# Row maxima of the global scores carried as eight more contraction rows, with local and global units taken in turn

## What is computed

```python
x = x + pos_emb[:S]                          # of the layer norm of x
w = x.reshape(B, nW, WIN, H, hd)             # WIN = 128, so 2 windows; 16 heads of 16
local = softmax(einsum('bnqhd,bnkhd->bnhqk', w, w) * scale) @ w
comp = conv1d(x, conv_w, stride=4) + conv_b  # 64 compressed positions
gt = concat([comp, global_memory])           # 64 + 64 global positions
glob = softmax(einsum('bshd,bghd->bhsg', x, gt) * scale) @ gt
mix = sigmoid(concat([local, glob]) @ gate_w + gate_b)
out = (mix * local + (1 - mix) * glob) @ out_w + out_b
```

## Time and profile before

| | us |
|---|---|
| median of 3 runs | 1249.25 |
| lowest and highest of them | 1235.91, 1250.31 |
| profiled execution, its own time | 1245.38 |
| its span, first to last instruction | 1243.6 |
| self-attention, first scores to last projection | about 31.7 to 509 |
| cross-attention | about 510 to 804 |
| experts | about 804 to the end |

### The profile page before, as it was taken

How to read it: one execution, slowest core, us unless ns; L and a number is a source line. 1 busy time by engine, 2 the same in 40 slices (tenths; PEclk the granted TensorE clock), 3 DMA queues, 4 the chain that set the end, 5 groups by cost and what they waited for, 6 DMA issues and landing times.

```text
span 1243.6 us, 29954 instructions
## 1 busy us (share of the span) xinstructions
PE 1134.6 (91%) x11749; PEld 981.6 (79%) x11749; DVE 593.2 (48%) x1187; ACT 518.3 (42%) x833; POOL 542.7 (44%) x651
## 2 busy tenths in 40 slices
PE   3699999999999998799998988999979989999995
PEld 2578787878788787577776776799978889999995
DVE  1355556555556654578886868632313212122221
ACT  1355555554545554377775766621112111111110
POOL 6434343444344222244455555446553444444442
PEclk9699999999999999799999988999989999999998
DMA  6472634435261612266555664479885768888882
GB/s 206 133 183 68 162 93 118 128 83 156 56 168 52 172 54 79 77 166 179 150 128 129 156 155 124 154 212 224 215 201 177 217 207 222 248 235 237 247 231 47
DMA packets 207737, 194.29 MB, mean 156 GB/s; under 512 B 62746, under 2 KB 164863, under 8 KB 207600
## 3 DMA queue, kind: packets, MB, share of 16 engines
q1 hardware_dynamic: 189408, 170.86, 48.3%
q0 software_dynamic: 15840, 18.77, 8.5%
q10 hardware_dynamic: 2352, 2.75, 0.7%
HBM read 152.25 MB, written 40.08 MB: 155 GB/s over the span
## 4 chain that ended last, share of the span: by engine, by line
PE 31%; DMA 17%; DVE 4%; issue 2%; ACT 1%; SPq 1%; POOL 1%; POOLq 0%; DVEq 0%; ACTq 0%
PE ps_scores L1640 11%; DMA out<-y,slot_row 11%; PE ps_out L1658 6%; PE ps_turn L1509 3%; DMA out<-y,out_row 3%; PE ps_misc L1541 2%; PE ps_scores L1496 2%; PE ps_out L1521 2%; DMA q_stack<-q_scr 2%; DMA q_scr<-qp 1%; PE ps_misc L1462 1%; DVE y L2102 1%; PE ps_scores L1489 1%; PE ps_misc L1529 1%; PE ps_turn L1625 1%
## 5 line engine op out<-in xcount | busy, mean ns | idle before, releaser
L1640 PEld LDWEIGHTS ps_scores<-xgT,w 128*128 128x128 f32 x2272 | 265.8, 193 | 5.0 <-ACT xgT L1855 0.7
L1640 PE MATMUL ps_scores<-xgT,w 128*128 128x128 f32 x2272 | 267.3, 277 | 0.7 <-ACT xgT L1855 0.5
L792 ACT ACTIVATE sa_probs<-ps_scores 128x1024 f32<-128x1024 f32 x128 | 131.0, 1023 | 153.6 <-PE ps_scores L521 153.6
L1861 ACT ACTIVATE silu<-ps_scores 128x512 f32<-128x512 f32 x71 | 42.4, 597 | 354.3 <-PE ps_scores L1640 354.3
L1658 PE MATMUL ps_out<-w2s,gate 128*128 x560 | 137.4, 390 | 15.2 <-DVE y L2102 15.2
L2096 DVE TENSOR_TENSOR gate<-ps_scores,silu 128x512 f32<-128x512 f32 x71 | 49.0, 690 | 180.9 <-ACT silu L1861 180.8
L1391 POOL DMA_INDIRECT out<-y,out_row x46 | 72.9, 1584 | 128.2 <-DMA out<-y,out_row 83.4
L1658 PEld LDWEIGHTS ps_out<-w2s,gate 128*128 128x128 f32 x560 | 103.1, 194 | 30.3 <-issue 18.8
L946 DVE TENSOR_REDUCE sa_rowmax<-ps_scores 128x8 bf16<-128x1024 f32 x64 | 78.4, 1224 | 77.4 <-PE ps_scores L507 77.4
L946 DVE TENSOR_REDUCE sa_rowmax<-ps_turn 128x8 bf16<-128x1024 f32 x64 | 78.4, 1225 | 57.5 <-PE ps_turn L512 56.9
L2102 DVE TENSOR_SCALAR y<-ps_out,slot_share 128x256 f32<-128x256 f32 x70 | 33.8, 483 | 133.4 <-DMA out<-y,slot_row 79.7
(11 more groups left out here) (265 smaller groups left out, 2093.4 us busy)
## 6 DMA issues: line engine op xcount, KB each, us to landing
w<-in_w1T SPq DMA_DIRECT2D x71, 512.0 KB, 3.9
w<-in_w3T SPq DMA_DIRECT2D x71, 512.0 KB, 4.9
q_stack<-q_scr SPq DMA_DIRECT2D x96, 128.0 KB
qs<-w_scr SPq DMA_DIRECT2D x24, 256.0 KB, 4.1
ks<-w_scr SPq DMA_DIRECT2D x24, 256.0 KB, 3.9
k_stack<-k_scr SPq DMA_DIRECT2D x48, 120.0 KB, 3.9
w_scr<-wp SPq DMA_DIRECT2D x7, 768.0 KB, 3.7
q_scr<-qp SPq DMA_DIRECT2D x14, 384.0 KB, 4.6
```

The lines of the kernel that those rows point to most:

```text
L792: act.activation(probs[s % 2][:], m.scores[s % 2][:], ACT.Exp, scale=SCALE).then_inc(exped, 1)
L1640: mm = pe.matmul(h_ps[r % 2][:, j, c, :], w13[r % 3][:, j, k, c * P:(c + 1) * P], xgT[r % 2][:, k, :], start=(k == 0), stop=(k == DT - 1))
```

## The change

For global units the order of the two products is turned round. `queries_scores` makes only the product for the maxima, in `turn`. DVE takes the maxima into `rowmax[1]`, now 32 columns wide of which eight are filled. `turn_max` is one matmul with those 32 columns as weights and minus the identity moving. It leaves minus the maxima, turned, on partitions 96 to 127 of the first 128 columns of `scores[1]`. `copy_max` on ACT writes them as bf16 onto eight more rows (96 to 103) of the stacked queries, the 8 x 128 block repeated for each of the eight heads, which is 8 x 1024 elements. `keys_scores` then makes the transposed scores with 104 rows of contraction. The same eight rows of `gs` hold, once and for all, a pattern that picks the head's own maximum, filled by POOL at the start (two copies of 8 x 3072 elements). `subtract_max` stays for the local units.

Units now alternate: n = s // 4, f = s // 2 % 2, kind = s % 2. So `scores[0]` is for local units only and `scores[1]` for global ones, `out` holds both kinds of one half, `outT` gets four buffers, and `turn_back` gathers from two of them. Because `turn` is now in use every second unit, steps that use its halves move: `turn_back(b-1,1,0)` goes behind `keys_scores(b,1)`, `keys_values` stands directly ahead of `queries_scores(b,5)`, `turn_back(b,0,0)` goes two units later. To make room in memory, `mixT` shares `diffT` and `memory` shares a tile of `att`.

Its core, with "..." where lines are left out:

```diff
+    rowmax = [sb(f"sa_rowmax{i}", [P, n], BF16) for i, n in enumerate((HU, 32))]
+    outT = [sb(f"sa_outT{i}", [P, 4, P]) for i in range(4)]
     wk, wv = (sb(n + "_sb", [P, DT, D]) for n in ("WkT", "WvT"))
...
             if p > 1:
-                sp.wait_ge(scored, R * UPR * (p - 1))
+                sp.wait_ge(shifted, R * UPR * (p - 1))
...
+        for i in range(2):
+            pool.wait_ge(pool_set, 10 + i)
+            pool.tensor_copy(gs[i][KS:, :, :].rearrange("j (f h) g -> j f h g", f=DT),
+                             m.ident[KS:KX_ROWS, KS:KX_ROWS].unsqueeze(1).unsqueeze(3).broadcast_to((HU, DT, HU, GK)))\
+                .then_inc(pool_set, 1)
+        pool.wait_ge(pool_set, 12)
         pool.wait_ge(rest_in, N_REST)
         pool.tensor_scalar(gate_b[:], gate_b[:], 0.5, None, ALU.mult).then_inc(bias_set, 1)
...
             n, kind, f = unit(s)
             p, r, U = b // R, b % R, UPR * b + s
             i = p % 2
-            ps = m.scores[s % 2]
...
             if s == 0 and b == 0:
                 for loaded in row0_stacked:
                     pe.wait_ge(loaded, 64)
             elif s == 0:
                 for loaded in w_stacked:
                     pe.wait_ge(loaded, 64 * p + 64)
-            if s == 2:
+            if U > 1:
+                pe.wait_ge(exped, U - 1)
+            for h in range(HU):
+                mm = pe.matmul(m.scores[0][:, h, :], ks[i][:, f * HU + h, r, n * P:(n + 1) * P],
+                               qs[i][0:KS, f * HU + h, r, n * P:(n + 1) * P], start=(h % 4 == 0), stop=False,
+                               skip_group_check=True)
+            mm.then_inc(scored, 1)
+
+        def queries_scores(b, s):
+            n, kind, f = unit(s)
+            p, r, U = b // R, b % R, UPR * b + s
+            i = p % 2
+            if s == 1:
                 for loaded in g_stacked:
                     pe.wait_ge(loaded, 32 * p + 32)
             if U > 1:
+                pe.wait_ge(maxed, U - 1)
+            for h in range(HU):
+                mm = pe.matmul(m.turn[:, h, :], qs[i][0:KS, f * HU + h, r, n * P:(n + 1) * P],
+                               gs[i][0:KS, f * HU + h, r * G:r * G + P], start=(h % 4 == 0), stop=(h % 4 == 3),
+                               skip_group_check=True)
+            mm.then_inc(scored, 1)
+
+        def turn_max(b, s):
+
+            U = UPR * b + s
+            pe.wait_ge(maxed, U + 1)
+            if U > 1:
                 pe.wait_ge(exped, U - 1)
+            else:
+                pe.wait_ge(pool_set, 12)
+            pe.matmul(m.scores[1][KS:, 0, :], rowmax[1][:], m.neg_ident[:], start=True, stop=True,
+                      tile_position=(0, KS), skip_group_check=True).then_inc(max_turned, 1)
+
+        def keys_scores(b, s):
+            n, kind, f = unit(s)
+            p, r = b // R, b % R
+            i = p % 2
+            pe.wait_ge(max_copied, global_unit(b, s) + 1)
             for h in range(HU):
-                mm = pe.matmul(ps[:, h, :], keys(h), queries(h), start=(h % 4 == 0), stop=False,
+                mm = pe.matmul(m.scores[1][:, h, :], gs[i][:, f * HU + h, r * G:r * G + P],
+                               qs[i][:, f * HU + h, r, n * P:(n + 1) * P], start=(h % 4 == 0), stop=(h % 4 == 3),
                                skip_group_check=True)
-            if kind:
-                pe.wait_ge(maxed, U)
-                for h in range(HU):
-                    mm = pe.matmul(m.turn[:, h, :], queries(h), keys(h), start=(h % 4 == 0), stop=(h % 4 == 3),
-                                   skip_group_check=True)
-            mm.then_inc(scored, 1)
+            mm.then_inc(shifted, 1)
 
         def subtract_max(b, s):
 
 
             pe.wait_ge(maxed, UPR * b + s + 1)
             for h in range(HU):
-                mm = pe.matmul(m.scores[s % 2][:, h, :], rowmax[s % 2][:, h:h + 1].broadcast_to((P, P)),
+                mm = pe.matmul(m.scores[0][:, h, :], rowmax[0][:, h:h + 1].broadcast_to((P, P)),
                                m.neg_ident[:], start=False, stop=(h % 4 == 3), skip_group_check=True)
             mm.then_inc(shifted, 1)
 
...
         def turn_back(b, n, kind, bank):
-            o = OPR * b + 2 * n + kind
-            pe.wait_ge(out_copied, o + 1)
-            for g in range(4):
-                mm = pe.transpose(bank[:, g * P:(g + 1) * P], outT[kind][:, g, :], m.ident[:])
+            pe.wait_ge(out_copied, OPR * b + 2 * n + 2)
+            for f in range(2):
+                for g in range(2):
+                    mm = pe.transpose(bank[:, (2 * f + g) * P:(2 * f + g + 1) * P], outT[2 * n + f][:, 2 * kind + g, :],
+                                      m.ident[:])
             mm.then_inc(back_made, 1)
 
         def turn_att(b, n, bank):
...
             if some:
-                scores(b, 1)
+                if old:
+                    pe.wait_ge(att_read, NT * (b - 1) + 1)
+                else:
+                    pe.wait_ge(mem_read, 1)
+                    pe.wait_ge(wT_read, 2)
+                queries_scores(b, 1)
                 subtract_max(b, 0)
             if more:
                 if old:
@@ -621,18 +669,11 @@
                     pe.wait_ge(gT_read, 1)
                 turn_c(b + 1, m.misc)
             if old:
-                turn_back(b - 1, 1, 0, side[1])
                 values(b - 1, UPR - 1)
 
             if some:
-                if old:
-                    pe.wait_ge(att_read, NT * (b - 1) + 1)
-                    pe.wait_ge(back_read, OPR * (b - 1) + 3)
-                else:
-                    pe.wait_ge(mem_read, 1)
-                    pe.wait_ge(wT_read, 2)
                 scores(b, 2)
-                subtract_max(b, 1)
+                turn_max(b, 1)
             if nxt or last and even:
                 pe.wait_ge(cT_read, b + 2)
                 if even:
@@ -644,9 +685,15 @@
                 cross_queries(1)
             if some:
                 values(b, 0)
-
-            if some:
-                scores(b, 3)
+                keys_scores(b, 1)
+                pe.wait_ge(maxed, UPR * b + 2)
+            if old:
+                turn_back(b - 1, 1, 0, side[1])
+
+            if some:
+                if old:
+                    pe.wait_ge(back_read, OPR * (b - 1) + 3)
+                queries_scores(b, 3)
                 subtract_max(b, 2)
             if old:
                 if (nxt or last) and even:
...
-                subtract_max(b, 3)
+                turn_max(b, 3)
             if old:
                 turn_att(b - 1, 1, m.misc)
+            if some:
+                values(b, 2)
+                keys_scores(b, 3)
             if (nxt or last) and even:
                 turn_w(b + 3, side[1])
             if more:
                 keys_values(b + 1, side[0])
-            if some:
-                values(b, 2)
-
-            if some:
-                scores(b, 5)
-                subtract_max(b, 4)
-            if old:
-                gate(b - 1)
+
             if some:
                 if more:
                     pe.wait_ge(k_read, b + 2)
                     pe.wait_ge(v_read, b + 2)
-                turn_back(b, 0, 0, side[0])
-                values(b, 3)
-
-            if some:
-                pe.wait_ge(back_read, OPR * b + 1)
                 if (nxt or last) and even:
                     pe.wait_ge(wT_read, b + 4)
+                queries_scores(b, 5)
+                subtract_max(b, 4)
+            if old:
+                gate(b - 1)
+            if some:
+                values(b, 3)
+
+            if some:
                 scores(b, 6)
-                subtract_max(b, 5)
+                turn_max(b, 5)
+                turn_back(b, 0, 0, side[0])
+                values(b, 4)
+                keys_scores(b, 5)
             if (nxt or last) and even:
                 if old:
                     pe.wait_ge(tanh_done, DT * b)
...
                 else:
                     cross_queries(0)
-            if some:
-                values(b, 4)
-
-            if some:
-                scores(b, 7)
+
+            if some:
+                pe.wait_ge(back_read, OPR * b + 1)
+                queries_scores(b, 7)
                 subtract_max(b, 6)
                 if nxt and even:
                     pe.wait_ge(conv_read, p + 2)
@@ -716,14 +764,13 @@
             if more:
                 scores(b + 1, 0)
             if some:
-                subtract_max(b, 7)
-            if old:
-                if some:
-                    pe.wait_ge(back_read, OPR * b + 2)
+                turn_max(b, 7)
+                values(b, 6)
+                pe.wait_ge(back_read, OPR * b + 2)
+                turn_att(b, 0, side[0])
+                keys_scores(b, 7)
+            if old:
                 project(b - 1)
-            if some:
-                turn_att(b, 0, side[0])
-                values(b, 6)
 
     def scalar_program(act):
...
             act.activation(probs[s % 2][:], m.scores[s % 2][:], ACT.Exp, scale=SCALE).then_inc(exped, 1)
 
```

(95 more changed lines are left out.)

22 lines of the change are left out of this document (11 added, 11 removed).

## The result

Over 20 runs each, the changed kernel took 1254.6 us (1246.2 to 1294.4) and the kernel before 1244.0 us (1234.3 to 1269.6). The ratio is 1.0091, with a 95% interval from 1.0066 to 1.0117: 11 us slower, and within 2%. The profiled execution of the changed kernel was an unusually long one: its experts took 461 us against 437 before, and no instruction of them is touched, so of its 39 us more than before only the self-attention is read here.

What follows compares the result with a forecast made beforehand. The prediction took TensorE to bound the kernel. Removed work of -25 us, added waits of +33 and the start's +3 gave +11 us, so 1260 us from a median of 1249.25; whole range 1237 to 1276.

Steps and rivals of the forecast that it cites:

- The bound: Self-attention stage: TensorE bounds it, with 1.8 us of waiting in a row of 28.5.
- The gain of 25 us: Global units: eight subtract_max matmuls become one, 1.57 us a row, 25 us over 16 rows.
- The copy: copy_max on ACT: taken at 1.02 us, like the exponential of 1024 from the same tile.
- The 0.6 and the 1.23: Bounds on copy_max: the cast of 512 elements, 0.61 us, below; two of those, 1.23, above.
- The waits: TensorE's waits in the new order: 3.7 us an even row, 4.0 an odd, against 1.3 and 2.3.
- three direct ones: Waits with nothing between: queries_scores(b,3) 0.9 us, queries_scores(b,5) 0.8, turn_back(b,0,0) 0.5.
- The start: POOL's two fills, 2.9 us each, delay the first global keys' split and store; 3.2 us lost in full.
- The sum: Whole kernel: -25 + 33 + 3 = +11 us, giving 1260 us.
- That the copy is dearer: Rival on copy_max: each 0.1 us more costs 4.8 us over 16 rows; 1287 at 1.5 us; chance 0.11.
- That waits absorb each other: Rival on TensorE's waits: they stay at 1.8 us a row, the gain comes through, 1227; chance 0.12.
- That the clock falls: Rival on TensorE's clock: one row in four at 1.2 GHz costs 48 us, 1308; chance 0.03.

Runs made afterwards that it cites:

- all three: Changed kernel with turn_back(b-1,1,0) ahead of values(b,0), subtract_max(b,4) and values(b,3) ahead of queries_scores(b,5), fills later; ratio to the kernel before 0.9895, again 0.9817.
- copy twice: Changed kernel with ScalarE's copy of the maxima issued twice and keys_scores waiting for the second; ratio to the kernel before 1.0668.

## Why the prediction was right, point by point

- **The bound.** TensorE, with waits that decide. Right: waits that were covered came back as time about one for one, and the gains at two places added up to 0.01 us.
- **The gain of 25 us.** The matmuls are gone, 56 ns each, as priced. As a sum by itself it was too large: on the kernel before, the removal alone gives 1.04 us a row instead of 1.57. How much of that lost cover is in the waits that the prediction lists for the new order, no run separates.
- **The copy.** Taken at 1.02 us, measured 1.004 on all 64. The 0.6 and the 1.23 that bounded it were both wide. The Trainium skill ("ScalarE: Activation LUTs", What ACT_TABLE_LOAD costs) gives 186 ns and 0.833 ns an element for an ACTIVATE with immediate scale and bias, an estimated 1.04 us for 1024 elements. The trace's 1.004 us, of a cast on 8 partitions, lies 3% below it.
- **The waits.** Read from start to start in the pair shown, in the order of the prediction's list: 0.3 (said 0.5), 0 and 0.2 (0.2 and 0.4), 0.9 (0.9), 0.2 (0.2), 0 (0.2), 0.8 (0.8), 0.3 (0.5), and 0.25 with 0.2 (0.2 with 0.2). Of the three direct ones, those ahead of `queries_scores(b,3)` and `queries_scores(b,5)` were right, and the one ahead of `turn_back(b,0,0)` was too long: of its 0.3 only 0.2 is a wait, by the step below. Most of those behind a queue were too long by 0.2 each. They sum to 2.9 and 3.1 us a row, where 3.7 and 4.0 were forecast (the listed terms of the odd row add up to 3.9, not 4.0, which changes the total by under 1 us).
- **The term that was mis-sized**: `turn_max` at 0.06 us. With the step to 32 weight columns and back it costs 0.26 where full-width blocks stand on both sides, and some 0.1 where a values block follows. Moved blocks pay such steps too: a values block behind the gate now starts 232.80 - 229.19 = 3.61 us after it, where `turn_back` stood 3.51 behind. The rows of the kernel before showed the step already, and I did not price it: `values` starts 0.54 us behind `subtract_max` (202.15 to 202.69 in the earlier trace rows), where a full-width block starts after 0.45. By the balance of a row the work that I had not counted comes to about 1.1 us (0.86 lost, plus the 1.57 removed, less some 1.3 of waits added). In the even row shown 1.0 can be read as such steps: 0.2 each at units 1 and 3, 0.1 each at units 5 and 7 and behind the gate, and 0.14 behind each of two turns that now stand ahead of a values block (the context's took 0.36 to the next start where it took 0.22, `turn_att` 0.59 where it took 0.45). Against it stand 0.85 us of waits too many. So 0.86 us a row was lost in the middle of the stage, not 0.5. That the sum came out all the same is owed to the two ends of the stage.
- **The start.** 2.78 us a fill, said 2.9, and the keys stored at 32.26, said 32.6. TensorE met them 2.1 us later than before (41.41 against 39.28), said 3.2. But by row 2 only 0.9 us of delay is left (98.44 against 97.50). In the kernel before, ScalarE stood for the store of the first cross keys and TensorE idled 4.2 us there, then worked at half clock (the next compression took 5.07 us to its end, in the changed kernel 4.05). In the changed kernel TensorE came there later, hardly waited, and kept its clock.
- **The end.** Not forecast: 4.4 us gained by the clock, next section.
- **The sum.** +11 us forecast, +8.0 in the self-attention of the trace (510.67 to 518.65), +11 in the runs. The 1260 us forecast are 5 above the 1254.6 measured because the kernel before, at 1249.25 in three runs, had a median of 1244.0 in twenty. In the trace: start +0.9, twelve rows +10.4, last rows and end -3.3. Without the clock's 4.4 at the end it would have been +12.4 there. So that the sum came out to the microsecond is partly luck.
- **The rivals.** That the copy is dearer: it wasn't, but the doubled copy shows that the price was right: 4.0 us a row for 1.0 us of copy, where the rival's sum gives 3.8, with the clock's 1.4 us in one row of three on top. That waits absorb each other: no, where they are direct pairs. That the clock falls: not here, but with 4.0 us more waiting a row it did in some rows.

## What to carry over

When TensorE is the bound and work is taken from it, walk its queue and list for each wait what stands between the releasing block and the waiting one. A pair with nothing between costs its full latency each time (1.4 us for a turn, a division and the restart, 2.7 for a block and its two copies), and here three of these (0.8, 0.8 and 0.2 us a row) took more than the 1.04 us a row that the removal gives by itself. Such waits are cheap to mend: moving a few blocks and the two fills turned 0.9% slower than the kernel before into 1 to 2% faster. Measure the repeated stage from start to start in the trace, where a tenth of a microsecond shows, and not only the whole run, which scattered by 1% and more.

## What the runs showed of the hardware that was not expected

- Going from matmuls with 128 weight columns to ones with 32, and back, costs TensorE about 0.1 us each way. The block ahead took 0.55 us to the next start instead of 0.45, the lone matmul 0.16 to the next full-width block and 0.00 to a block of its own form, and a second one 0.04. A lone matmul with 128 columns among such blocks took 0.06. The matmuls with 32 columns also write to only 32 partitions, and no run tells the two apart.
- The clock at the end of the stage is a matter of luck. The last gate and the last projection, the same 16 and 8 matmuls behind the same waits, in the kernel before and in the changed one:

```profile
496.74 6.49 PE L563 MATMUL ps_misc<-attT,gate_w 128*128 128x256 f32 x16 [0.68 <-ACT attT L806]
505.61 3.64 PE L571 MATMUL ps_misc<-out_w,mixT 128*128 128x256 f32 x8 [2.38 <-DVE mixT L968]
```

```profile
509.14 3.72 PE L606 MATMUL ps_misc<-attT,gate_w 128*128 128x256 f32 x16 [0.67 <-ACT attT L859]
515.24 1.99 PE L614 MATMUL ps_misc<-out_w,diffT 128*128 128x256 f32 x8 [2.38 <-DVE diffT L1027]
```


  They took 6.49 + 3.64 us at the lower level and 3.72 + 1.99 at the upper one, after the same 0.7 and 2.4 us of idling. In the other traces it was the one or the other, one of each, or something between. The same kernel, *all three*, had 5.41 us for its last gate in one trace and 3.72 in the other, so I count these 4 us to no change.
- TensorE not busy for 8% of twelve rows (28.4 of 351.7 us) cost no clock. In *copy twice* the clock fell behind two waits of 1.19 and 0.81 us with a little work between them in one row, and behind the same two waits in another row it did not. What decides, the runs don't tell.
